# Attention output kept transposed, with inverse sums spread through DRAM and channels placed by transfers

## The reference

```python
x = x + _L0_conv_ref(_ln_c(x), ...)          # attention
    q, k, v = (qkv[0], qkv[1], qkv[2])       # each (b * heads, n, hd)
    bias = (rel_h[:, :, :, :, None] + rel_w[:, :, :, None, :]).reshape(b * heads, n, n)
    attn = jax.nn.softmax(jnp.einsum('bnd,bmd->bnm', q * scale, k) + bias, axis=-1)
    out = jnp.einsum('bnm,bmd->bnd', attn, v)
    out = out.reshape(b, heads, n, hd).transpose(0, 2, 1, 3).reshape(b, n, dim)
    out = out @ proj_w.T + proj_b
t = t + _L0_ffn_ref(_ln_t(t), ...)           # one expert for each token
```

## Time and profile before

| | |
|---|---|
| device time, median of 3 runs | 880.63 us (878.61 to 881.58) |
| the profiled execution | 887.1 us, of which the span from first to last instruction 884.8 us |
| mean granted clock of TensorE | 0.941 |
| TensorE busy | 785.4 us, 89% of the span |
| VectorE busy | 724.5 us, 82% |
| ScalarE busy | 608.8 us, 69% |
| GpSimd busy | 284.8 us, 32% |
| attention | to about 646 us |
| `gate`, and sorting after it | from about 646 to about 735 us |
| experts | the rest |

### The profile page before, as it was taken

How to read it: one execution, slowest core, us unless ns; L and a number is a source line. 1 busy time by engine, 2 the same in 40 slices (tenths; PEclk the granted TensorE clock), 3 DMA queues, 4 the chain that set the end, 5 groups by cost and what they waited for, 6 DMA issues and landing times. The chain is left out here.

```text
span 884.8 us, 32156 instructions
## 1 busy us (share of the span) xinstructions
PE 785.4 (89%) x11946; PEld 487.2 (55%) x11946; DVE 724.5 (82%) x1022; ACT 608.8 (69%) x1139; POOL 284.8 (32%) x437
## 2 busy tenths in 40 slices
PE   3999938999999999999999999999988617999994
PEld 1768802444444444444444444444478617999994
DVE  6876767998999999999999999899347485888883
ACT  3675605888888888888888888888845603544442
POOL 5530000023343423303232233421015304666662
PEclk9999956999999999999999999999989657999998
DMA  6255973345555545444454545543044402222310
GB/s 175 72 144 176 365 225 101 101 126 135 137 145 139 134 128 135 125 120 129 135 137 132 140 135 145 150 125 84 4 179 133 166 0 75 81 82 83 97 57 8
DMA packets 69738, 109.71 MB, mean 124 GB/s; under 512 B 20139, under 2 KB 36681, under 8 KB 68146
## 3 DMA queue, kind: packets, MB, share of 16 engines
q1 hardware_dynamic: 59120, 75.49, 30.5%
q0 software_dynamic: 9248, 26.51, 10.6%
q10 hardware_dynamic: 1314, 6.95, 2.1%
HBM read 77.58 MB, written 33.19 MB: 125 GB/s over the span
## 5 line engine op out<-in xcount | busy, mean ns | idle before, releaser
L913 DVE TENSOR_REDUCE neg_max<-max_ps 128x1 f16<-128x1024 f32 x384 | 451.9, 1221 | 41.6 <-PE max_ps L762 33.9
L896 ACT ACTIVATE probs<-ring_ps 128x512 f32<-128x512 f32 x768 | 413.7, 596 | 68.7 <-PE ring_ps L796 60.0
L796 PE MATMUL ring_ps<-q_side,k_side 113*32 113x512 f16 x3072 | 241.1, 386 | 11.6 <-DMA q_side<-rel_split 8.3
L808 PE MATMUL out_ps<-probs,values 128*32 128x256 f32 x3072 | 200.4, 380 | 0.2 <-ACT probs L896 0.2
L762 PE MATMUL max_ps<-k_side,q_side 48*128 48x256 f16 x1536 | 137.5, 280 | 18.0 <-ACT ident L871 9.3
L808 PEld LDWEIGHTS out_ps<-probs,values 128*32 128x32 f32 x3072 | 92.7, 110 | 70.9 <-issue 1.0
L796 PEld LDWEIGHTS ring_ps<-q_side,k_side 113*32 113x32 f16 x3072 | 73.2, 94 | 96.8 <-ACT probs L896 38.7
L658 POOL COPY max_copies<-neg_max 128x32 f16<-128x32 f16 x48 | 10.1, 210 | 350.4 <-DVE neg_max L913 350.4
L762 PEld LDWEIGHTS max_ps<-k_side,q_side 48*128 48x128 f16 x1536 | 49.1, 95 | 121.9 <-issue 70.1
L1467 PE MATMUL hid_ps<-slot_t,w_top 128*118 128x128 f16 x312 | 69.0, 221 | 0.8 <-ACT slot_t L1513 0.8
L1468 PE MATMUL hid_ps<-slot_t,w_top 128*118 128x128 f16 x312 | 68.8, 221 | 0.0
(11 more groups left out here) (230 smaller groups left out, 1357.0 us busy)
## 6 DMA issues: line engine op xcount, KB each, us to landing
q_side<-rel_split SPq DMA_DIRECT2D x384, 64.0 KB, 2.3
q_side<-qk_split SPq DMA_DIRECT2D x192, 64.0 KB, 2.5
rel_split<-expert_weights ACTq DMA_DIRECT2D x6, 1024.0 KB, 4.9
rel_split<-expert_weights SPq DMA_DIRECT2D x6, 1024.0 KB, 6.1
q_side<-qk_split SPq DMA_DIRECT2D x48, 128.0 KB, 2.8
k_side<-qk_split SPq DMA_DIRECT2D x144, 32.0 KB, 1.8
token_rows<-tn_parts SPq DMA_DIRECT2D x8, 512.0 KB, 3.4
expert_weights<-in_w_t POOLq DMA_DIRECT2D x32, 117.2 KB, 3.0
```

The source lines that it names most:

```text
L796: last = nc.tensor.matmul(ring_ps[turn_of(k) % BANKS][at:at + COLS, :], k_side[slot(s)][:, tile * P + at:tile * P + at + COLS], queries, s ...
L808: last = nc.tensor.matmul(out_ps[quarter * 2 * HD:(quarter + 1) * 2 * HD, :], values[j][:, tile, :], probs[:, u % 2 * GROUP + 2 * i + quar ...
L896: nc.scalar.activation(probs[:, u % 2 * GROUP + i, :], ring_ps[turn_of(k) % BANKS][:], ACT.Exp).then_inc(exp_done, 1)
L913: nc.vector.tensor_reduce(neg_max[:, j % 2, t:t + 1], max_ps[t % 2][:], AX, ALU.max, negate=True).then_inc(tile_max, 1)
```

## The change

The output of a head stays as `out_ps` has it, with channels on the partitions, up to the projection, which wants it so. `turn_out` and `normalize` go, and so do `turn_attention` and `copy_attention` in `gate`. `values` is filled with ones first, so that the row of sums is still made. `out_t` has two buffers. For head n:

1. SyncE stores the 4 rows of sums of `out_t` to DRAM (`store_sums`) and loads them as 128x8 (`load_sums`).
2. VectorE takes the reciprocal (`invert_sums`).
3. SyncE stores it to DRAM (`store_inverse`) and, when it has landed, loads each quarter's row onto 16 partitions (`spread_inverse`, 4 transfers).
4. GpSimd multiplies `out_t` with it (`scale_output`).
5. SyncE moves each quarter to its channels and queries in `att_t` (`place_output`, 4 transfers, SBUF to SBUF).

SyncE's step of head s does the placement of head s-3, the inverse of head s-2 and the sums of head s-1. Its heads are all written out now. The last two heads are finished in `gate`: `project_out` waits for an image's placements. The row of ones for the projection's bias is set by GpSimd in head 19, `w3_whole` and `w3_parts` lie in `att_t` before that, and the W3 splits run in every second head, not in every fifth.

```diff
+def store_sums(sp, g, n):
+    sp.wait_ge(g.out_copied, n + 1)
+    sp.dma_start(g.sums_dram[n % 2], g.out_t[HD::2 * HD, n % 2, :]).then_inc(g.sums_stored[n % 2], 16)
+def load_sums(sp, g, n):
+    sp.wait_ge(g.sums_stored[n % 2], 16 * (n // 2 + 1))
+    sp.dma_start(g.sums[:, n % 2, :], g.sums_dram[n % 2].rearrange("q n -> (q n)").rearrange("(p c) -> p c", p=P)).then_inc(g.sums_loaded[n % 2], 16)
+def invert_sums(nc, dve, g, slot, head, reused):
+    dve.wait_ge(g.sums_loaded[slot % 2], 16 * (B // 2 * head + slot // 2 + 1))
+    if reused:
+        dve.wait_ge(g.inverse_stored[slot % 2], 16 * (B // 2 * head + slot // 2))
+    nc.vector.reciprocal(g.inverse[:, slot % 2, :], g.sums[:, slot % 2, :]).then_inc(g.inverted, 1)
+def store_inverse(sp, g, n):
+    sp.wait_ge(g.inverted, n + 1)
+    sp.dma_start(g.inverse_dram[n % 2].rearrange("q n -> (q n)").rearrange("(p c) -> p c", p=P), g.inverse[:, n % 2, :]).then_inc(g.inverse_stored[n % 2], 16)
+def spread_inverse(sp, g, n):
+    sp.wait_ge(g.inverse_stored[n % 2], 16 * (n // 2 + 1))
+    for q in range(4):
+        sp.dma_start(g.spread[2 * HD * q:2 * HD * q + HD, n % 2, :],
+                     g.inverse_dram[n % 2, q:q + 1, :].broadcast_to([HD, N // 4])).then_inc(g.inverse_spread[n % 2], 16)
+def scale_output(nc, pool, g, n):
+    pool.wait_ge(g.inverse_spread[n % 2], 64 * (n // 2 + 1))
+    if n >= 2:
+        pool.wait_ge(g.placed[(n - 2) % B], 64 * ((n - 2) // B + 1))
+    nc.gpsimd.tensor_tensor(g.scaled[:, n % 2, :], g.out_t[:, n % 2, :], g.spread[:, n % 2, :], ALU.mult).then_inc(g.output_scaled, 1)
+def place_output(sp, g, n):
+    sp.wait_ge(g.output_scaled, n + 1)
+    head, image = n // B, n % B
+    at, c = head * HD % C, head * HD // C
+    for q in range(4):
+        queries = slice(image * N + q * N // 4, image * N + (q + 1) * N // 4)
+        sp.dma_start(g.att_t[at:at + HD, c, queries], g.scaled[2 * HD * q:2 * HD * q + HD, n % 2, :]).then_inc(g.placed[image], 16)
...
+                if s.before(3):
+                    place_output(sp, g, s.n - 3)
+                if s.before(2):
+                    store_inverse(sp, g, s.n - 2)
+                if s.before(1):
+                    store_sums(sp, g, s.n - 1)
                 if s.after(1):
                     store_max(s.n + 1, slot(s, 1))
+                if s.before(2):
+                    spread_inverse(sp, g, s.n - 2)
+                if s.before(1):
+                    load_sums(sp, g, s.n - 1)
                 if s.after(3):
                     load_positions(sp, g, head(s, 3), slot(s, 3))
 
-            steps(sp, BH, SLOTS, step)
+            sp.wait_ge(g.spread_set, 1)
+            for n in range(BH):
+                step(Step(n, n // SLOTS, n % SLOTS, BH, True))
...
-                nc.gpsimd.tensor_copy(values[slot(s)][:, :, 0:VW], g.v_sb[:, head(s) + slot(s) * HEADS]).then_inc(values_ready, 1)
+                nc.gpsimd.tensor_copy(values[slot(s)][:, :, 0:HD], g.v_sb[:, head(s) + slot(s) * HEADS]).then_inc(values_ready, 1)
                 if s.after(1):
                     repeat_max(s.n + 1, slot(s, 1), s.before(1))
+                if s.before(2):
+                    scale_output(nc, pool, g, s.n - 2)
...
+                if n == W3_UNTIL:
+                    pool.wait_ge(g.w3_stored, 16 * EXPERTS)
+                    pool.wait_ge(max_repeated, n + 2)
+                    pool.wait_ge(g.output_scaled, n - 1)
+                    nc.gpsimd.memset(g.att_t[C:C + 1, 1, :], 1.0).then_inc(g.ones_row_set, 1)
+                    pool.wait_ge(g.ones_row_set, 1)
...
-            def turn_out(n):
-                pe.wait_ge(out_copied, n + 1)
-                picked = g.ident[:].rearrange("p (q c) -> p q c", q=QUARTERS)[:, :, 0:VW]
-                for b in range(2):
-                    for at in range(0, P, COLS):
-                        last = nc.tensor.matmul(turned_ps[at:at + COLS, b, :, :], out_t[:, b * P + at:b * P + at + COLS], picked,
-                                                start=True, stop=True, skip_group_check=True, tile_position=(0, at))
-                last.then_inc(turned, 1)
...
-                    if u == 2 and s.before(1):
-                        bank_free(s, TURNED_AT)
-                        turn_out(s.n - 1)
...
-            def copy_out(n, reused):
+            def copy_out(n, j, reused):
                 act.wait_ge(group_done, PAIR_TILES * (n + 1))
                 if reused:
-                    act.wait_ge(turned, n)
-                nc.scalar.activation(out_t[:], out_ps[:], ACT.Copy).then_inc(out_copied, 1)
+                    act.wait_ge(g.output_scaled, n - 1)
+                nc.scalar.activation(g.out_t[:, j % 2, :], out_ps[:], ACT.Copy).then_inc(g.out_copied, 1)
...
-            def normalize(n, at, j, reused):
-                dve.wait_ge(turned, n + 1)
-                by_tile = turned_ps.rearrange("p b q c -> p q b c")
-                if reused:
-                    dve.wait_ge(att_done, n)
-                nc.vector.reciprocal(recip[:].rearrange("p (q b) -> p q b", b=2), by_tile[:, :, :, HD]).then_inc(recip_done, 1)
-                dve.wait_ge(recip_done, n + 1)
-                dst = g.att_sb[:, j * KT:(j + 1) * KT, bass.ds(HD * at, HD)].rearrange("p (q b) d -> p q b d", b=2)
-                by = recip[:].rearrange("p (q b o) -> p q b o", b=2, o=1).broadcast_to([P, QUARTERS, 2, HD])
-                nc.vector.tensor_tensor(dst, by_tile[:, :, :, 0:HD], by, ALU.mult).then_inc(att_done, 1)
...
-                    if u == 2 and s.before(1):
-                        normalize(s.n - 1, head(s, -1), slot(s, -1), s.before(2))
+                    if u == 0 and s.before(2):
+                        invert_sums(nc, dve, g, slot(s, -2), head(s, -2), s.before(4))
...
+            last, before = BH - 1, BH - 2
+            place_output(sp, g, before - 1)
+            store_inverse(sp, g, before)
+            store_sums(sp, g, last)
+            spread_inverse(sp, g, before)
+            load_sums(sp, g, last)
+            place_output(sp, g, before)
...
+                if b == 1:
+                    store_inverse(sp, g, last)
+                    spread_inverse(sp, g, last)
+                if b == 2:
+                    place_output(sp, g, last)
...
-            def turn_attention(s):
-                if s:
-                    pe.wait_ge(at_ready, 2 * s)
-                for c in range(2):
-                    for i in range(TPS):
-                        last = nc.tensor.transpose(at_ps[c][:, i * P:(i + 1) * P], g.att_sb[:, TPS * s + i, c * C:(c + 1) * C], g.ident[:])
-                    last.then_inc(at_ps_ready, 1)
             def project_out(s):
-                pe.wait_ge(at_ready, 2 * s + 2)
+                pe.wait_ge(g.placed[s // 2], 64 * HEADS)
...
```

## The result

The changed kernel takes 1075.70 us (median of 4 runs, 1072.89 to 1078.09), the kernel before 879.62 us beside it: **1.2207 times the time, with a 95% interval from 1.2163 to 1.2251**. It is slower by 196 us where 246 were forecast. The first view is the table of waits (engine, line, what it waited for: us in total, times, longest us), the two rows on SPq from the waits of SyncE's queue.

A forecast was written before the change was run, and what follows sets the result against it. SyncE's issue queue was taken to bound the loop: 16.4 us per full head against 10.55, +246 over 42 heads, +250 for the loop, -3 for the stage after, giving 1127 us; range 1000 to 1200.

The forecast's parts named there:

- What bounds the kernel: Attention loop: SyncE's queue, waiting only 1.8 us per 10.34 us head, gets 11 more transfers and sets the pace.
- The head of SyncE: SyncE's full head in the loop: 28 transfers and a wait, 14.66 us, plus 1.7 of fetching, 16.4 us.
- the fetch of code: SyncE's written-out heads: instruction-fetch stalls of 0.062 us per transfer, 28 transfers, 1.7 us per head.
- many more than 36: Instruction-fetch queue q8: the changed kernel's profile would show many more than the 36 fetches before.
- the rows decide: Fetch term: charged from trace rows against the skill's rule, which would give nothing and some 73 us less.
- wait for the inverse to land: SyncE's step before the spreads: a wait of 0.9 us per head, between 0.4 and 2.4 us.
- a landing of the inverse that is covered: Listed sign of a wrong forecast: SyncE would not have to wait for the stored inverse, booked at 0.9 us.
- GpSimd: GpSimd's product behind the spread, ahead of weight splitting: at most some tenths of a us in 8 heads.
- A: Rival, SyncE's queue: the 11 transfers fit its waiting at 0.17 us or less each, 851 us; 5%.
- B: Rival, SyncE's queue: small transfers cost half (0.21 us), fetching and the wait nothing, about 920 us; 5%.
- D: Rival, loop: idle gaps lower TensorE's clock, period 18.5 us or more, above 1205 us; 6%.
- The stage after: Projection after the loop: transposes go but heads 46 and 47 are placed late; -3 us, between -8 and +6.

The follow-up runs named there:

- d1: Kernel before with SyncE's heads written out, plus 11 idle 16x128 stores per full head on SyncE that nobody waits for: 1019.17 us, ratio 1.1578.
- s1: Changed kernel with the inverse spread by one transfer over 128 partitions instead of four over 16 each: 1022.81 us, ratio 1.1603.
- v1: Changed kernel with the sums spread from DRAM by one transfer and inverted in place by VectorE, all 128x256: 955.23 us, ratio 1.0807.
- v4: v2 with the reciprocal cut to 8 of the 256 columns, so most output is multiplied with the sum: 880.42 us, ratio 0.9995.
- u1: Kernel before with SyncE's 48 heads written out, nothing else changed: 882.08 us, ratio 0.9993.
- w1: Changed kernel with GpSimd's product of the output moved behind the pieces of weight splitting: 1068.26 us, ratio 1.2091.
- v2: v1 with the 4 placements of a head issued by GpSimd, not SyncE: 917.68 us, ratio 1.0378.
- p1: Changed kernel with the 4 placements of a head issued by GpSimd right behind its product: 1035.55 us, ratio 1.1751.
- v5: v3 with the one-transfer spread issued by GpSimd instead of SyncE: 996.62 us, ratio 1.1298.
- v3: v2 with a small reciprocal before the spread; GpSimd loads sums and stores the inverse, SyncE spreads a step later: 997.55 us, ratio 1.1338.
- v6: v3 with the spread as four transfers over 16 partitions each instead of one: 963.77 us, ratio 1.0918.

## Why the prediction was right, and by how much its steps were not

**What bounds the kernel.** Right. SyncE was said to have 1.8 us of slack, to be overfilled by 11 issues, and to be waited for by TensorE at the positions. d1 shows that with idle transfers, s1 and v1 by taking some away: 28, 25 and 23 on SyncE give 14.2, 12.8 and 12.0 us. With 19 in v4 the head is 10.2 us and SyncE waits again, 45.3 us in 40, so there it is no longer the limit. The count of waits was right (45, forecast 40) and their length less (2.9 us mean, forecast 5).

**The head of SyncE.** Forecast 16.4 us, measured 14.87 as a mean of 42 and 14.2 in the steady part. The term that was mis-sized most is the fetch of code, 1.7 us per head. The changed kernel has long issues, but nearly all in its first heads:

```profile
187.35 3.13 SPq L521 DMA_DIRECT2D k_side<-qk_split  x3
...
201.34 1.90 SPq L537 DMA_DIRECT2D q_side<-rel_split  x1
```

In the first 443 us of the full heads the issues that overran by more than 0.3 us did so by some 11 us in all (6 in the kernel before and in u1), where the term booked 42 x 1.7 = 71. I took a rate from the only heads that were written out, which were also the first of the attention, and spread it over all. q8, the queue of instruction fetches, has 34 packets in the changed kernel (36 before), so the change didn't bring more of them either, where "many more than 36" was forecast. The rule of the Trainium skill, "Runtime: NRT & Kernel Launch", section on instruction fetch mechanics, that fetching straight code is mostly hidden, agrees with u1 (882.08 against 882.32 us) and with the heads after 270 us; "the rows decide" was the wrong choice, because the rows could not tell written-out heads from early ones. Without that term the forecast would have been 1127 - 42 x 1.7 = 1056, 20 us below the measured time and still in the range: the range is wide enough for either, and the hit says little of the fetch.

**The other terms of a head**, forecast and measured in the head at 390.45 and in steady ones: 8 loads of products 3.72 and 3.7 to 4.0; 4 placements 1.88 and 2.47, since the transfer from SBUF to SBUF issues in 0.6, above the upper bound of 0.55 that I took; store of the inverse 0.63 and 0.62; store of the sums 0.47 and 0.58; wait for the inverse to land 0.9 and mostly nothing; 4 spreads 1.88 and 1.8 to 2.0; load of the sums 0.63 and 0.46; 8 positions 4.00 and 3.75. The wait is the second step that failed: "a landing of the inverse that is covered" stood among the signs of being wrong, and it is covered in 39 of 45 heads. The landing took 1.6 us at the median, under the 2.0 of the nearest row, and SyncE comes to the wait 1.75 us after it began to issue the store (396.88 to 398.63). The sum 14.66 comes near 14.2 by luck: the wait was too dear by about as much as the placements and the store of the sums were too cheap. The mean of 14.87 holds slower early heads: the 14 up to 390.45 us took 15.56 us each, the 28 behind them 14.52.

**GpSimd.** Booked at some tenths in 8 heads. Measured 19.9 us of waits before the maxima in 16 heads, of which w1 takes back 7 to 10. The mechanism was seen and its size was not: in the head shown under w1 the product starts 13.0 us into SyncE's step (314.87 to 327.90), where 12 was booked, and the copy of the maxima behind the splits comes 4.5 us into the next (335.41 against 330.87).

**Rivals.** A (a price of 0.17 us per transfer) and B (small ones at half price) are refuted by d1's 0.46. The shortest issue of SyncE in the changed kernel's loop took 0.30 us, most took 0.42. D (the clock) happened in part: the granted clock is 0.87 in the loop, so TensorE is busy 78% of it and not 60%, and its 11.6 us per head stay below SyncE's 14.2. What the clock costs is small but not nothing. In the head behind the one shown, TensorE resumes at 408.63 at the lower level, and the maxima can be stored 5.0 us later, where it was 3.1 before (405.32 to 408.41); SyncE stood 1.0 us for them:

```profile
408.63 1.04 PE L868 MATMUL ring_ps<-q_side,k_side 113*32 113x512 f16 x8 [5.11 <-DMA q_side<-rel_split]
...
413.31 0.27 ACT L935 ACTIVATE max_rows<-ring_ps 32x128 f16<-32x128 f32 x1 [0.98 <-PE ring_ps L859]
...
413.60 0.53 SPq L672 DMA_DIRECT2D q_side<-max_rows  x1
```

Such waits are within the 19.9 us before the maxima; how much of them is the clock's and how much GpSimd's is not separated.

**The stage after.** Forecast -3, measured +6.7 (from the last matmul of values to the first matmul of the experts' stage 97.6 us, 90.9 before), just beyond the bound of +6.

```profile
826.35 1.07 PE L880 MATMUL out_ps<-probs,values 128*32 128x256 f32 x16 [0.20 <-ACT probs L954]
834.06 0.98 PE L1131 MATMUL proj_ps<-proj_w_top,att_t 96*128 96x192 f32 x2 [6.64 <-PEq L622]
...
844.88 0.59 PE L1131 MATMUL proj_ps<-proj_w_top,att_t 96*128 96x192 f32 x2 [2.65 <-DMA att_t<-scaled]
```

The transposes are gone, but TensorE waits 6.64 us at the barrier between the stages, so the projection starts no sooner (6.6 us after the last matmul, 6.3 before), and then waits for head 46. What holds the barrier is open. In v1, v2 and v4, where SyncE's queue has nothing of the last sums left but their store, the same wait is 0.91 us; in p1 and w1 it is 4.5 and 6.3. It isn't SyncE's queue alone: in v5 that queue is as short and the wait is 9.5 us, with the load of the sums and the store of the inverse on GpSimd, and in v3 and v6, which have them there too, 11.8 and 11.3. No run tries it apart.

## What to carry to other kernels

When one queue issues all transfers of a loop, count its instructions and multiply: a busy share isn't shown for it, and every transfer costs its issue however small it is. Before spending transfers, set them against the most that they can bring: here up to 0.55 us per head was in sight, v4, where the queue no longer holds the loop, shows 0.1 of it (10.2 us against 10.3), and the 11 transfers cost 181 us in the full heads. A rate read from the first heads of a stage is a rate of first heads; look for the same event in the steady part before charging it everywhere.

## What the runs showed of the hardware

- An issue on SyncE, written out, occupied it for 0.42 us (0.47 to the next) with 4 KB, 16 KB, 64 KB and 128 KB alike; with SBUF on both sides 0.6. The number of partitions doesn't order the dearer ones: the load of the sums onto 128 took 0.42, their store from 4 took 0.53, and the store of the inverse from 128 took 0.58 in the changed kernel, behind the placements, and 0.42 in p1 (460.76), without them. On GpSimd one took 0.48 to 0.60, and the one of 128 KB 0.71 (p1, v5).
- One load of 128 KB over 128 partitions landed 4.7 us after its issue (v5), four of 16 KB 1.6 us each in the changed kernel and 2.2 in v6; three issues more bought 34 us (v3, v6).
- VectorE's reciprocal took 0.19 us for 8 values per partition (v4) and 1.74 for 256 (v2), as much as 1.4 maxima over 1024.
- TensorE busy 78% of a stretch, with a gap in every head, had a mean granted clock of 0.87 (changed, 171.4 to 614 us); busy 98% it had 1.00 (before).
- 11 idle transfers per head moved TensorE's waits for positions from 7.7 us (u1) to 96.2 us.
